# A token mixer with eight experts on one core: the experts' two products, half products by Strassen's scheme

## What is computed

```python
def _L0_ffn_ref(x, centroids, ln_g, ln_b, w1, b1, w2, b2):
    ...
    def balanced_assignment(scores):
        T, E = scores.shape
        C = T // E
        taken = jnp.zeros((T,), dtype=bool)
        parts = []
        for e in range(E):
            s = jnp.where(taken, -jnp.inf, scores[:, e])
            _, idx = jax.lax.top_k(s, C)
            parts.append(idx)
            taken = taken.at[idx].set(True)
        return jnp.concatenate(parts)
    ...
    norm = layer_norm(feat, ln_g, ln_b)
    scores = jax.lax.stop_gradient(norm @ centroids.T)
    sort_by_expert = balanced_assignment(scores)
    routed = feat[sort_by_expert].reshape(E, C, D)
    h = layer_norm(routed, ln_g, ln_b)
    h = jax.nn.gelu(jnp.einsum('ecd,edf->ecf', h, w1) + b1[:, None, :])
    ...
```

## Time and profile before

| | us |
|---|---|
| median of three runs | 5907.34 |
| lowest and highest | 5901.49, 5909.01 |
| profiled execution, its own time | 5900.49 |
| its span, first to last instruction | 5898.6 |
| mean granted clock of TensorE | 0.972 |

### The profile page before, as it was taken

One profiled execution on the slowest core, in us unless ns is written; L12 is line 12 of the kernel. 1 busy time (PEld: TensorE's weight loads), 2 busy tenths in 40 slices (PEclk: granted clock), 3 DMA queues, 4 the chain that ended last, 5 costly groups with the idle time before them and its releaser, 6 DMA issues. The chain is left out here.

```text
span 5898.6 us, 243936 instructions
## 1 busy us (share of the span) xinstructions
PE 5437.2 (92%) x110664; PEld 3805.1 (65%) x110664; DVE 3741.3 (63%) x9004; ACT 2014.6 (34%) x3659; POOL 1396.8 (24%) x1156
## 2 busy tenths in 40 slices
PE   6999999999989999899999999975999999999998
PEld 6777777777777777777777777752444444444443
DVE  6788888788888788878888888845232232232310
ACT  4444444444444444444444444420000000000000
POOL 1222222222222222222222222212022022121220
PEclk9999999999999999999999999987999999999999
DMA  1001000010100000010000000003112112112110
GB/s 62 23 18 25 18 21 22 18 25 18 25 18 23 21 20 24 18 25 18 23 20 23 21 20 23 16 16 97 61 50 93 50 52 102 50 52 99 39 64 14
DMA packets 108638, 211.07 MB, mean 36 GB/s; under 512 B 25553, under 2 KB 26705, under 8 KB 107089
## 3 DMA queue, kind: packets, MB, share of 16 engines
q1 hardware_dynamic: 92240, 144.91, 8.4%
q0 software_dynamic: 15360, 50.48, 2.6%
HBM read 144.60 MB, written 50.72 MB: 33 GB/s over the span
## 5 line engine op out<-in xcount | busy, mean ns | idle before, releaser
L392 DVE COPY_PREDICATED time_raw<-time_known,w_bank 128x96 f32<-128x96 int32 (+6 forms) x3072 | 816.7, 274 | 214.0 <-PE w_bank L1043 128.5
L1862 PE MATMUL moe_bank<-moe_w,moe_hidden 128*128 128x512 f32 x2048 | 930.4, 597 | 0.0
L1849 PE MATMUL moe_bank<-moe_hT,moe_w 128*128 128x512 f32 x2048 | 924.3, 594 | 1.5 <-DVE moe_hT L1743 1.5
L1764 ACT ACTIVATE moe_hidden<-moe_bank,moe_b 128x512 f32<-128x512 f32 x256 | 175.9, 687 | 1635.3 <-PE moe_bank L1849 1635.3
L1849 PEld LDWEIGHTS moe_bank<-moe_hT,moe_w 128*128 128x128 f32 x2048 | 386.5, 190 | 471.7 <-issue 469.8
L1862 PEld LDWEIGHTS moe_bank<-moe_w,moe_hidden 128*128 128x128 f32 x2048 | 379.8, 190 | 429.7 <-issue 428.2
L909 POOL TENSOR_TENSOR time_grow<-time_eye,time_grow 128x512 f32<-128x512 f32 x256 | 371.7, 1452 | 1131.6 <-DVE time_grow L418 1131.6
L1028 PE MATMUL w_bank<-time_ew,time_grow 32*32 32x64 f32 x32768 | 403.8, 218 | 160.4 <-issue 143.6
L1028 PEld LDWEIGHTS w_bank<-time_ew,time_grow 32*32 32x32 f32 x32768 | 350.7, 104 | 199.4 <-issue 157.2
L1043 PE MATMUL w_bank<-time_keys,time_queries_u 32*32 32x160 f32 x8192 | 362.5, 309 | 31.5 <-issue 20.3
L1743 DVE COPY moe_hT<-moe_bank 128x512 f32<-128x512 f32 x64 | 44.2, 691 | 501.0 <-PE moe_bank L1834 501.0
(11 more groups left out here) (226 smaller groups left out, 9421.5 us busy)
## 6 DMA issues: line engine op xcount, KB each, us to landing
moe_w<-in_w SPq DMA_DIRECT2D x64, 1024.0 KB, 7.4
mid_xn<-time_xn_rows SPq DMA_DIRECT2D x128, 129.0 KB, 2.5
time_x_rows<-in_x SPq DMA_DIRECT2D x128, 128.0 KB, 2.7
time_base<-in_x SPq DMA_DIRECT2D x128, 128.0 KB, 3.0
mid_acc<-time_mixed SPq DMA_DIRECT2D x128, 128.0 KB, 2.4
mid_scores<-time_rated SPq DMA_DIRECT2D x128, 2.0 KB, 1.7
moe_b<-in_b SPq DMA_DIRECT2D x8, 256.0 KB, 12.8
time_key_w<-in_w_key_w SPq DMA_DIRECT2D x1, 1024.0 KB, 5.3
```

What stands on the lines that cost most here:

```text
L392: e.copy_predicated(by_raw[:, "uy".index(q), n0:n1, :, 0:8 * j + 8], known[:, "uy".index(q), :, :, mine].to_broadcast([P, n1 - n0, 2, 8 * ...
L1764: e.activation(hidden[now % 4][:, :], up[now % 3][:, :], ACT.Gelu_apprx_tanh, bias=b1[:, x * FC + k:x * FC + k + 1]).then_inc(act.sem, act ...
L1849: got = e.matmul(up[now % 3][:, :], w1[:, g * F + k * P:g * F + (k + 1) * P], hT[x % 2][:, g * CAP + half * HALF:g * CAP + (half + 1) * HA ...
L1862: got = e.matmul(down[t][:, :], hidden[now % 4][:, t * P:(t + 1) * P], tile(w2, k), start=k == 0, stop=k == FC - 1)
```

## The change

The two products of an expert are computed by one level of Strassen's scheme (in Winograd's form): each of tokens, inner channels and outer channels is cut in two, and seven products of halves, P1 to P7, stand for eight. The work is now in 16 segments of 512 tokens, two to an expert, the even one first. For widening, a segment has four units (q): each gives 2 x 2 tiles of 128 hidden channels for 2 x 256 tokens. For narrowing it has the seven products once, over the eight tiles of each half. All matmuls of the two products have 256 columns. Each of the seven products has its place in TensorE's order, P1, P6, P2, P7, P5, P4, P3 for a unit and P1, P4, P5, P6, P2, P7, P3 for the narrowing; P2, P7 (and in the widening P3) add to a bank that is already filled.

- Sums of the weights: GpSimd makes four sums of each unit of w1 (128x512, `w1_sums`), and of each half of w2 (128x1024, `w2_sums`). Those of w1 for the next expert stand at the end of its odd segment, those of w2 in the even segment itself, after the stores and around the gather of the sums so far. Those of w1 for expert 0 stand ahead of its first gather.
- Sums of the rows: VectorE makes four sums of 128x512 from the transposed rows (`turned_sums`).
- In a unit: ScalarE copies P1 from its bank; VectorE makes five sums (U2, U3, C22, C21, C12) with a bank as one input; ScalarE applies gelu in eight pieces of 128x256 (C22 and the like in place).
- Ahead of and during the narrowing: VectorE makes four sums of 128x2048 from the hidden rows (sum_c, diff_a, diff_d, diff_b), and ten of 128x512 for the results.
- The rows of a segment are scaled by VectorE in one instruction (128x512) with one buffer `h`; gain and bias are applied by ScalarE after the transpose (`keep`, four instructions of 128x128 to a tile, `kept`).
- The choice of the next expert is cut into pieces that VectorE takes one at a time (`choose`) between the sums of the present expert's even segment (all twelve counts) and of its odd one (the places). A piece ends with what the next count needs and begins with that count's reading. TensorE has the counts behind P6 and P5 of each unit and behind the first five products of the narrowing. Before the even segment's first unit VectorE runs the first piece.
- Loads: w1 in four parts by unit, w2 in four quarters, each as soon as the odd segment of the expert before is done with it, which for the last quarter of w2 is the segment's end. gain and bias are loaded as one number for each partition and group.

The diff, cut to its core:

```diff
+    SEG = 2 * E
+    ST = KT // 2
+    HT, HD, HF, HC = ST * P // 2, C // 2, F // 2, C // 2
+    UNITS_ = HF // HC
+    HK = HF // P
...
+        up_of = {"P1": ("a", w1_of(0, 0), hT_of(0, 0)), "P6": ("b", s_of(2), tt_of(2)), "P2": ("a", w1_of(0, 1), hT_of(1, 0)),
+                 "P7": ("b", w1_of(1, 0), hT_of(0, 1)), "P5": ("c", s_of(1), tt_of(1)), "P4": ("d", w1_of(1, 1), tt_of(4)),
+                 "P3": ("c", s_of(4), hT_of(1, 1))}
+        down_of = {"P1": ("e", "11", w2_of(0, 0)), "P4": ("f", "22", t_of(4)), "P5": ("g", "21", t_of(1)),
+                   "P6": ("h", "11", t_of(2)), "P2": ("e", "12", w2_of(1, 0)), "P7": ("h", "22", w2_of(0, 1)),
+                   "P3": ("e", "12", w2_of(1, 1))}
+        UP, DOWN = tuple(up_of), tuple(down_of)
...
+        def turned_sums(e, s):
+            half = lambda k, j: hT[k][:, 2 * j * HT:2 * (j + 1) * HT]
+            e.wait_ge(act.sem, act[f"kept{s}.{ST - 1}.{G - 1}"])
+            e.tensor_tensor(hT_t[1][:, :], half(1, 0), half(0, 0), ALU.subtract).then_inc(dve.sem, dve.step(f"T1.{s}"))
+            e.wait_ge(dve.sem, dve[f"T1.{s}"])
+            e.tensor_tensor(hT_t[2][:, :], half(1, 1), hT_t[1][:, :], ALU.subtract).then_inc(dve.sem, dve.step(f"T2.{s}"))
+            e.tensor_tensor(half(1, 0), half(1, 1), half(1, 0), ALU.subtract).then_inc(dve.sem, dve.step(f"T3.{s}"))
+            e.wait_ge(dve.sem, dve[f"T2.{s}"])
...
+        def up_sums(e, s, q, choice):
+            even, odd = s % 2 == 0 and routes(s), s % 2 == 1 and routes(s)
+            e.wait_ge(act.sem, act[f"P1.{s}.{q}"])
+            e.wait_ge(pe.sem, pe[f"up{s}.{q}.P6"])
+            if q:
+                e.wait_ge(dve.sem, dve[f"C12.{s}.{q - 1}"])
+            elif s:
+                e.wait_ge(dve.sem, dve[f"acc12.{s - 1}"])
+            e.tensor_tensor(second[:, :], first[:, :], up["b"][:, :], ALU.add).then_inc(dve.sem, dve.step(f"U2.{s}.{q}"))
+            choose(choice, even or odd and q < 2)
+            e.wait_ge(pe.sem, pe[f"up{s}.{q}.P7"])
+            e.tensor_tensor(third[:, :], first[:, :], up["b"][:, :], ALU.add).then_inc(dve.sem, dve.step(f"U3.{s}.{q}"))
+            e.wait_ge(pe.sem, pe[f"up{s}.{q}.P5"])
+            e.wait_ge(dve.sem, dve[f"U3.{s}.{q}"])
+            e.tensor_tensor(unit(hid["22"], q), third[:, :], up["c"][:, :], ALU.add).then_inc(
+                dve.sem, dve.step(f"C22.{s}.{q}"))
+            choose(choice, even and q < 3 or odd and q < 3)
+            e.wait_ge(pe.sem, pe[f"up{s}.{q}.P4"])
+            e.tensor_tensor(unit(hid["12"], q), third[:, :], up["d"][:, :], ALU.subtract).then_inc(
+                dve.sem, dve.step(f"C21.{s}.{q}"))
+            e.wait_ge(pe.sem, pe[f"up{s}.{q}.P3"])
+            e.tensor_tensor(unit(hid["21"], q), second[:, :], up["c"][:, :], ALU.add).then_inc(
+                dve.sem, dve.step(f"C12.{s}.{q}"))
...
+        def down_sums(e, s, choice):
+            even, more, last = s % 2 == 0 and routes(s), s + 1 < SEG, UNITS_ - 1
+            e.wait_ge(act.sem, act[f"H21.{s}.{last}.1"])
+            e.tensor_tensor(hid["21"][:, :], hid["21"][:, :], hid["22"][:, :], ALU.add).then_inc(
+                dve.sem, dve.step(f"sum_c{s}"))
...
+            e.tensor_tensor(hid["11"][:, :], hid["21"][:, :], hid["11"][:, :], ALU.subtract).then_inc(
+                dve.sem, dve.step(f"diff_a{s}"))
+            choose(choice, even)
...
+            e.wait_ge(pe.sem, pe[f"down{s}.P2"])
+            e.tensor_tensor(hid["12"][:, :], hid["12"][:, :], hid["11"][:, :], ALU.subtract).then_inc(
+                dve.sem, dve.step(f"diff_b{s}"))
+            e.wait_ge(pool.sem, pool[f"summed{s}.{ST - 1}"])
+            e.tensor_tensor(acc_of(0, 0), acc_of(0, 0), in_bank(down["e"]), ALU.add).then_inc(dve.sem, dve.step(f"acc11.{s}"))
+            if more:
+                turned_sums(e, s + 1)
+            choose(choice, even)
+            e.wait_ge(pe.sem, pe[f"down{s}.P7"])
+            e.tensor_tensor(third[:, :], first[:, :], down["h"][:, :], ALU.add).then_inc(dve.sem, dve.step(f"half3.{s}"))
...
+            e.wait_ge(pe.sem, pe[f"down{s}.P3"])
+            e.tensor_tensor(second[:, :], second[:, :], down["e"][:, :], ALU.add).then_inc(dve.sem, dve.step(f"out12.{s}"))
+            e.wait_ge(dve.sem, dve[f"out12.{s}"])
+            e.tensor_tensor(acc_of(0, 1), acc_of(0, 1), in_bank(second), ALU.add).then_inc(dve.sem, dve.step(f"acc12.{s}"))
...
+                if s:
+                    store(e, s - 1)
+                if s % 2 == 0:
+                    w2_sums(e, x, 0)
+                if s:
+                    e.wait_ge(core.stored, 16 * ST * s)
                 for t in tiles:
-                    if x:
-                        e.wait_ge(dve.sem, dve[f"result{x - 1}.{t}"])
...
+                if s % 2 == 0:
+                    w2_sums(e, x, 1)
+                e.wait_ge(b2_in, 16 * (x + 1))
...
+        def w1_sums(e, x, q):
+            e.wait_ge(w1_in[q], 32 * (x + 1))
+            at = slice(q * HC, (q + 1) * HC)
+            a11, a12, a21, a22 = (w1_of(i, j)[:, :, at] for i in range(2) for j in range(2))
+            s1, s2, s4 = (s_of(n)[:, :, at] for n in (1, 2, 4))
...
+            e.tensor_tensor(s1, a21, a22, ALU.add).then_inc(pool.sem, pool.step(f"w1_S1.{x}.{q}"))
+            e.wait_ge(pool.sem, pool[f"w1_S1.{x}.{q}"])
+            e.tensor_tensor(s2, s1, a11, ALU.subtract).then_inc(pool.sem, pool.step(f"w1_S2.{x}.{q}"))
+            e.wait_ge(pool.sem, pool[f"w1_S2.{x}.{q}"])
+            e.tensor_tensor(s4, a12, s2, ALU.subtract).then_inc(pool.sem, pool.step(f"w1_S4.{x}.{q}"))
+            e.tensor_tensor(a21, a11, a21, ALU.subtract).then_inc(pool.sem, pool.step(f"w1_S3.{x}.{q}"))
...
+                even, odd = s % 2 == 0 and routes(s), s % 2 == 1 and routes(s)
+                for q in units:
+                    widen(e, s, q, "P1")
+                    widen(e, s, q, "P6")
+                    if even:
+                        if s and q == 0:
+                            e.wait_ge(dve.sem, dve[f"acc12.{s - 1}"])
+                        route.on_tensor(e, s // 2 + 1, 2 * q, count_bank)
+                    elif odd and q in (1, 2):
+                        if q == 1:
+                            e.wait_ge(dve.sem, dve[f"U2.{s}.0"])
+                        route.on_tensor(e, s // 2 + 1, 10 + 2 * q, count_bank)
+                    widen(e, s, q, "P2")
+                    widen(e, s, q, "P7")
+                    widen(e, s, q, "P5")
+                    if even and q < 3:
+                        route.on_tensor(e, s // 2 + 1, 2 * q + 1, count_bank)
+                    elif odd and q in (1, 2):
+                        route.on_tensor(e, s // 2 + 1, 11 + 2 * q, count_bank)
+                    widen(e, s, q, "P4")
+                    widen(e, s, q, "P3")
+                for i, p in enumerate(DOWN):
+                    narrow(e, s, p, 0)
+                    if s + 1 < SEG and p in ("P6", "P2"):
+                        turn(e, s + 1, 1 if p == "P6" else 3)
+                    narrow(e, s, p, 1)
+                    if s + 1 < SEG and p in ("P5", "P6"):
+                        turn(e, s + 1, 0 if p == "P5" else 2)
+                    if even and i == 0:
+                        e.wait_ge(dve.sem, dve[f"sum_c{s}"])
+                    if even and i < 5:
...
+            for u in range(2):
+                for g in range(2):
+                    got = e.matmul(up[bank][:, u * HT:(u + 1) * HT], weight[:, g, (2 * q + u) * P:(2 * q + u + 1) * P], rows[:, g],
+                                   start=p not in UP_ADDS and u == 0 and g == 0, stop=g == 1, skip_group_check=True)
+            got.then_inc(pe.sem, pe.step(f"up{s}.{q}.{p}"))
...
+            for k in range(HK):
+                got = e.matmul(down[bank][:, u * HC:(u + 1) * HC], hid[part][:, k * HT + u * P:k * HT + (u + 1) * P], weight[:, k],
+                               start=p not in DOWN_ADDS and u == 0 and k == 0, stop=k == HK - 1, skip_group_check=True)
+            if u:
+                got.then_inc(pe.sem, pe.step(f"down{s}.{p}"))
...
```

More of the change, by code:

```diff
@@ L1647, in experts @@
         factor = lambda t: xn_rows[:, t * ROW + C:t * ROW + C + 1]
-        slot = lambda x, t: bass.IndirectOffsetOnAxis(ap=slots[:, x * KT + t:x * KT + t + 1], axis=0)
-        turn_bank = lambda x, t: spare if x or t >= FIRST else down[t]
-        hT_of = lambda x, t: hT[x % 2][:, :].rearrange("p (g t) -> p g t", g=G)[:, :, t * P:(t + 1) * P]
-        experts_, tiles, steps = range(E), range(KT), [(half, k) for half in range(2) for k in range(FC)]
-        LAST = len(steps) - 1
-        CONSTS = 16 * (4 + route.LOADS)
@@ new lines, in experts @@
+        dve.stage(row_names(0, *tiles) + t_names(0) + [n for s in segs for n in (
+            [f"{n}{s}.{q}" for q in units for n in ("U2.", "U3.", "C22.", "C21.", "C12.")]
+            + [f"sum_c{s}", f"diff_a{s}", f"diff_d{s}"] + row_names(s + 1, 0, 1, 2) + [f"half2.{s}"] + row_names(s + 1, 3)
```

(9 more changed lines are left out.)

711 lines of the change are left out of this document (416 added, 295 removed).

## The result

The changed kernel takes 5766.39 us, the median of four runs (5750.73 to 5777.60), against 5908.18 for the kernel before: a ratio of 0.9762, 95% interval 0.9744 to 0.9780. It is faster, by 142 us; the forecast was 5782, so 125 us. The profiled execution took 5777.6 us with a span of 5775.8.

A forecast was written before the change was run, and what follows sets the result against it. TensorE, busy 92% of the span, was taken as the bound. 5900.5 - 199 (matmuls) + 60 (even segments) + 14 (start and end) = 5775.5, with 0.12% on it 5782 us; range 5708 to 5880.

The forecast's parts named there:

- The records: Experts' matmuls on TensorE: 7168 records of 256 columns at 0.2175 us, 1559 us for 1758, a gain of 199 us.
- Rival (e): TensorE's matmuls: half-width records aren't half price, 0.403 us each, so the experts take 1130 us more; chance 0.03.
- The even segments: Seven routed even segments: TensorE waits 1.5 + 6.1 + 1.0 = 8.6 us in each, 60 us together.
- first piece: Start of each routed even segment: VectorE's first piece of the choice holds up the count behind P6, 1.5 us.
- w2 sums: Even widening: VectorE's pieces wait beside GpSimd's eight long w2 sums, making TensorE 5.7 us late after slack.
- short sums: Even segments: GpSimd's short sums delay a piece by 2.4 us, just over one unit's slack; 0.4 us in all.
- narrowing: Narrowing of routed even segments: VectorE's sums and row scaling are tightest there; 1 us put on each.
- (a): The forecast itself: TensorE remains the bound with short gaps in seven segments, 5740 to 5825 us; chance 0.50.
- The start: Before expert 0's first matmul: earlier loads, VectorE waits beside w1 and w2 sums, four gathers; together about +16 us.
- (b): Even segments: VectorE's waits fall into its idle time, 5716 us on the median, 5700 to 5740; chance 0.17.
- (c): Seven routed even segments: VectorE is the bound, 20.5 us each, 5872 us on the median, 5825 to 5895; chance 0.19.
- (d): Routed even segments: TensorE's gaps also lower its clock, 112 us more, 5984 us, slower than before; chance 0.08.

The follow-up runs named there:

- the second profile: The changed kernel run again with nothing altered; 5775.0 us, ratio 0.976 to the kernel before.
- e4: The kernel before the change with each 512-column matmul of the two products split into two of 256; 5928.57 us, ratio 1.0024.
- e2: The changed kernel with GpSimd's w2 sums cut to 2 of 256 columns and its b2 and xn sums to 8 columns; 5717.4 us, ratio 0.967.
- e1: The changed kernel with GpSimd's w2 sums cut to 2 of their 256 columns, the rest left out; 5737.8 us, ratio 0.970.
- e7: The changed kernel with three units' w1 sums and the first w2 sums held until the first piece of expert 1's choice is done; 5765.2 us, ratio 0.971.
- e11: The changed kernel with five counts in the even widening, seven in the even narrowing, first piece and next tile's scaling moved earlier; 5726.4 us, ratio 0.9676.
- e5: The changed kernel with the first piece of the next expert's choice run in the odd narrowing before; 5774.2 us, ratio 0.972.
- e6: The changed kernel with the choice spread: first piece earlier, one per even widening unit, five in the even narrowing, rest in the odd widening; 5792.0 us, ratio 0.976.

## Why the prediction was right

The sign, the bound and the mechanism held, and the time fell 16 us below the forecast. By the stage the forecast was -199 + 60 + 14 = -125 us, and -139.5 came out (-143.6 in the second profile).

- **The records.** 7168 records at 0.2158 us make 1547 us for 1758: -211 where the sum had -199. This is the term that was mis-sized. The straight line between 128 and 512 columns gave 0.2175, because the 0.112 of the earlier trace rows lies 5 ns above a fourth of 0.429 and the line carried 3 of them to 256 columns, where the record has 1.3. The record lies 1.7 ns below the line and 1.3 above the lower bound, half of 0.429. e4 shows the same from the other side. Rival (e) is out: no fixed part but 2.5 ns (its 0.213 us for the stream stands in no row; half of 0.429 is 0.2145). By the sustained pairs of the Trainium skill, "TensorE: Matmul & The Clock Gate" (section "Back-to-back issue gap") the change would have lost time. The trace disagrees: 0.2158 us for 0.429 is half, not three quarters.
- **The even segments.** Forecast 8.6 us each; six of them measured 8.7 in the widening (58.56 less 49.9) and nothing in the narrowing. The parts: first piece 1.5 (measured 1.5, e2), w2 sums 5.7 (6.1, e1, of which 4.1 waits and 2.0 clock), short sums 0.4 (1.0), narrowing 1.0 (0). A w2 sum took 2.35 us at its shortest and 2.5 in the mean, for the estimated 2.5. The sum of the first three is near by luck in one respect: gaps at the full clock make 6.7 us (the segments of 56.6 us), and what lifts the mean to 8.7 is the clock, which the forecast had left out of (a). Of the 52 us in the six, TensorE's idle time is 32.1 and the lower clock some 12; the other 8, a third of a us per gap, I can't place.
- **Where the long wait fell.** The largest gap stood in the period of the short sums, where the forecast had put 0.4 us. The piece there belongs to the lower half and has two more short steps (L1490, L1493), which the forecast had not counted; it was late already from the w2 sums, for with these short (e1) no wait is longer than 1.3 us.
- **The start.** Forecast +16, measured +12.0 to the first widening. Keys 2.9 earlier (2.5); choice 8.4 longer (10), in e7 with four w1 sums beside it for sixteen 2.0 longer; the wait for four gathers 8.04 us for 3.82 (4); scaling to first widening 2.2 longer, where 5 were set down for the w2 sums. Segment 0 then lost 16.9 us in its widening against some 5.4 before (3.39 of gap and 2 of clock), 11.5 more, where 8.6 stood: "the first count waits as it did before" was wrong, it waited 7.74 us. Together 23.5 for 24.6.
- **The end.** -1.5: from TensorE's last record to the end of the span 13.4 us for 15.0.
- **Rivals.** (b) is out, even segments are longer; by e11 it is what another order of the same work reaches. (c) is out: 8.7 and not 20.5, with gaps in three of the four units, where the forecast had the first two. The mechanism of (d) is there in small: after the 2.68 us gap the clock was at half for 6 us in the rows above, and it costs 3.3 us in such a segment (59.9 for 56.6). In the second profile two of six segments had it, in the first two in full, three in part and one not at all. The argument against (d), that the summed gaps are shorter than the 3.39 us of the row, did not hold: 2.68 us was enough, and in e5 1.66.

Against these terms, 52 for the six even segments, 23.5, -1.5 and -211 make -137; the other 2.5 us of the stage I can't place. What else stays open: why the same gap lowers the clock in one segment and not in another.

## What to carry to other kernels

When TensorE is full, moving sums to GpSimd is free on GpSimd and not on VectorE: price each as a wait of its own length for every short SBUF-only step that runs beside it, and cut it into shorter ones if a chain of such steps has to be on time. Short steps that fall where GpSimd only issues transfers don't pay this. Place an uninterruptible block of the side work by its contended length, in the stretch where both engines have room; e6 shows that moving the many small steps can carry the one long one into the wrong place. Judge by the stage that was changed when another stage varies by more than the effect.

## What the runs showed of the hardware

An fp32 record of 256 columns starts every 0.2158 us and one of 512 every 0.429, so splitting costs 2.5 ns for each further record (e4). Not only tiny steps wait for GpSimd: a 128x512 VectorE sum with all operands in SBUF took 3.08 us for 0.69 beside sums of 128x1024, while the same shape with a PSUM input kept its 0.68. Beside GpSimd's issuing of gathers `cand` kept its 0.23 us (e11). The granted clock fell to half behind a gap of 2.68 us, in some segments for 6 us and in others with the same gap not at all, and in e5 behind a gap of 1.66.
